# A two-layer transformer on one Trainium2 core: the first layer's feed-forward loads one per head, and sixteen matrix products whose results nobody reads

## What is computed

```python
x = x + L0_attn(layernorm(x))   # 16 heads of 128, rotary, signed weights (see below)
x = x + L0_ffn(layernorm(x))    # 16 experts, 4 per token, groups, plus a shared expert
x = x + L1_attn(layernorm(x))   # 16 heads of 16, rotary, softmax
x = x + L1_ffn(layernorm(x))    # 16 experts, 4 per token, plus a shared expert
# expert: silu(h @ g.T) * (h @ u.T) @ d.T, weighted by the routing weight of its token
```

## Time and profile before

| | us |
|---|---|
| median of 3 runs | 867.16 |
| lowest, highest run | 866.05, 870.68 |
| profiled execution | 864.81 |
| span of the profiled execution, first to last instruction | 863.1 |
| TensorE busy | 827.2 |

### The profile page before, as it was taken

One profiled execution on the slowest core, in us unless ns is written; L12 is line 12 of the kernel. 1 busy time (PEld: TensorE's weight loads), 2 busy tenths in 40 slices (PEclk: granted clock), 3 DMA queues, 4 the chain that ended last, 5 costly groups with the idle time before them and its releaser, 6 DMA issues.

```text
span 863.1 us, 14804 instructions
## 1 busy us (share of the span) xinstructions
PE 827.2 (96%) x4544; PEld 628.5 (73%) x4544; DVE 637.9 (74%) x1358; ACT 525.1 (61%) x1106; POOL 453.7 (53%) x391
## 2 busy tenths in 40 slices
PE   8899999999899999989998999999999989999997
PEld 7678888877688888866887888764444447888886
DVE  6798888888788888988476865768788644676553
ACT  4778788777678888863644533336566564454442
POOL 3555555555455556551666776623300426656774
PEclk9999999999999999999999999999999999999999
DMA  5232233333322333112665457412441122344451
GB/s 157 93 98 89 96 97 97 98 98 97 119 86 99 98 97 110 64 66 56 203 214 177 134 164 276 143 57 68 142 136 51 57 99 93 122 124 142 152 162 64
DMA packets 57442, 99.20 MB, mean 115 GB/s; under 512 B 8288, under 2 KB 19040, under 8 KB 57376
## 3 DMA queue, kind: packets, MB, share of 16 engines
q1 hardware_dynamic: 57376, 98.39, 35.7%
HBM read 71.88 MB, written 9.57 MB: 94 GB/s over the span
## 4 chain that ended last, share of the span: by engine, by line
PE 67%; DVE 10%; issue 9%; POOL 7%; ACT 3%; DMA 2%; SPq 0%; DVEq 0%; POOLq 0%; ACTq 0%
PE ps L993 10%; PE ps L979 9%; PE ps L970 9%; PE ps L321 7%; PE ps L387 5%; PE ps L335 5%; PE ps L348 4%; PE ps L375 3%; PE ps L362 3%; PE ps L1661 3%; POOL q_sin L542 2%; PE ps L1542 2%; PE ps L1631 2%; DVE nm L1853 2%; POOL wqk_lo L536 1%
## 5 line engine op out<-in xcount | busy, mean ns | idle before, releaser
L1117 POOL TENSOR_TENSOR ew_lo<-ew_raw,ew_hi 128x768 fp32r<-128x768 f32 x68 | 128.0, 1884 | 59.7 <-ACT ew_hi L1083 51.6
L1069 ACT ACTIVATE hid_hi<-guw 128x512 fp32r<-128x512 f32 x68 | 43.0, 632 | 156.5 <-POOL guw L1133 106.4
L1172 DVE TENSOR_TENSOR hid_lo<-guw,hid_hi 128x512 fp32r<-128x512 f32 x68 | 80.6, 1186 | 72.1 <-ACT hid_hi L1069 72.0
L1133 POOL TENSOR_TENSOR guw<-gu,cwb 128x512 f32<-128x512 f32 x61 | 80.4, 1318 | 91.1 <-issue 73.9
L542 POOL TENSOR_TENSOR q_sin<-q_sw,sin 128x512 f32<-128x512 f32 x62 | 80.4, 1305 | 79.6 <-DMA q_sw<-q_in 78.8
L1853 DVE TENSOR_REDUCE nm<-ps 128x1 f32<-128x512 f32 x128 | 81.3, 682 | 19.3 <-PE ps L1565 18.1
L1748 ACT ACTIVATE e<-ps 128x512 f32<-128x512 f32 x128 | 68.7, 602 | 35.2 <-PE ps L1661 35.0
L993 PE MATMUL ps<-ew_hi,hid_hi 128*128 128x256 f32 x272 | 78.3, 288 | 2.4 <-DVE hid_lo L1172 1.8
L497 DVE TENSOR_TENSOR q_rot<-ps,q_sin 128x512 f32<-128x512 f32 x64 | 43.9, 689 | 49.1 <-POOL q_sin L542 23.2
L438 ACT ACTIVATE ex<-sabs,nmax 128x512 f32<-128x512 f32 (+3 forms) x128 | 61.5, 553 | 28.2 <-DVE nmax L502 28.2
L993 PE MATMUL ps<-ew_lo,hid_hi 128*128 128x256 f32 x272 | 76.8, 283 | 0.0
(11 more groups left out here) (190 smaller groups left out, 2397.5 us busy)
## 6 DMA issues: line engine op xcount, KB each, us to landing
ew_raw<-in_ew SPq DMA_DIRECT2D x68, 384.0 KB, 3.5
q_sw<-q_in SPq DMA_DIRECT2D x128, 128.0 KB, 2.0
cwb<-cw_dram SPq DMA_DIRECT2D x61, 256.0 KB, 3.5
wqk_raw<-in_wqk SPq DMA_DIRECT2D x32, 256.0 KB, 2.7
wv_raw<-in_wv SPq DMA_DIRECT2D x32, 128.0 KB, 2.2
wo_raw<-in_wo SPq DMA_DIRECT2D x32, 128.0 KB, 2.2
qs<-stk_q SPq DMA_DIRECT2D x16, 256.0 KB, 3.7
ks<-stk_k SPq DMA_DIRECT2D x16, 256.0 KB, 4.1
```

The costliest lines, as they stand in the source:

```text
L1117: pool.tensor_tensor(ff[f].ew[1][:, i % EW_SLOTS, :], ew_raw[:, i % RAW_SLOTS, :], fp(ff[f].ew[0][:, i % EW_SLOTS, :]), ALU.subtract).then ...
L1133: pool.tensor_tensor(ff[f].guw[:, i % 2, :], ff[f].gu[:, i % 2, :], ff[f].cwb[:, r % CWB_SLOTS, :], ALU.mult).then_inc(sem("guw"), 1)
L1172: dve.tensor_tensor(ff[f].hid[1][:, i % 2, :], ff[f].guw[:, i % 2, :], fp(ff[f].hid[0][:, i % 2, :]), ALU.subtract).then_inc(sem("hid_lo"), 1)
```

## The change

The three small router transfers (`gw_raw`, `ebias`, `lower4`) are issued behind head 11 (H0 - 5) and not behind head 16; items 0, 1 and 2 are loaded behind heads 12, 13 and 14. For layer 1 `ffn_sp` does the same as before.

In layer 1's attention, sixteen `warm` products (128 rows, 128 columns, 512 moving columns, of `xT_hi`) are put in front of the score product of a slot: one in slot 3 of steps 21 to 24, three each in slots 1 and 2 of step 25, slot 2 of step 28 and slot 0 of step 29. Each group first waits, by `bank_wait`, for the bank that it writes: that of the slot's own maximum, of the transposed maxima (`taken`), of the logits (twice), and of the transposed routing weights (`cwT`).

```diff
         def a0_at_sp(sp, i):
-            if i == H0:
-                ffn_sp(sp, 0)
+            if i == H0 - 5:
+                ffn_sp_small(sp, 0)
+            if H0 - 4 <= i < H0 - 4 + RAW_SLOTS:
+                ew_load(sp, 0, i - (H0 - 4))
             if i == N0 - 3:
                 ew_load(sp, 0, RAW_SLOTS)
...
-        def ffn_sp(sp, f):
+        def ffn_sp_small(sp, f):
             sp.dma_start(gw_raw[:, :, :], a[f"gw{f}"]).then_inc(sem("gw_ld"), 16)
             sp.dma_start(ebias[:, :], a[f"ebias{f}"].partition_broadcast(P)).then_inc(sem("ebias_ld"), 16)
             sp.dma_start(lower4[:, :], a["lower4"].partition_broadcast(P)).then_inc(sem("ebias_ld"), 16)
+
+        def ffn_sp(sp, f):
+            ffn_sp_small(sp, f)
             for i in range(RAW_SLOTS):
                 ew_load(sp, f, i)
...
+        STEP_WARM = {(s, 3): ("max", HEADS * (s + LEAD) + 3) for s in (21, 22, 23, 24)}
+        STEP_WARM |= {(STEP_LOGIT, 1): ("taken", 7), (STEP_LOGIT, 2): ("logits", 0), (STEP_CWT, 2): ("cwT", 0),
+                      (STEP_CWT + 1, 0): ("logits", 0)}
...
                 for j in range(HEADS):
+                    if (s, j) in STEP_WARM:
+                        kind, n = STEP_WARM[s, j]
+                        bank_wait(pe, kind, n)
+                        warm(pe, 1 if kind == "max" else 3, BANK_OF[kind, n], half_of(xT_hi[:, 1, :], 1))
                     if HEADS * s + j + S_BANKS < HEADS * STEPS:
                         scores(HEADS * s + j + S_BANKS)
                     slot_pe(pe, s, j)
```

## The result

| | median of 20 runs (lowest to highest) | profiled execution | its span, mean granted clock |
|---|---|---|---|
| before | 870.83 us (861.31 to 876.05) | 864.81 us | 863.1 us |
| after | 864.67 us (860.60 to 867.33) | 863.15 us | 861.4 us, 0.996 |

The ratio is 0.9942, interval 0.9922 to 0.9962: 5.0 us faster (0.9942 x 870.83 = 865.8). The change is close to that; the time isn't: 864.67 was measured, and the kernel before is itself at 870.83 in more runs. That the change has the right size is luck: two errors stand against each other, as the traces show.

What follows compares the result with a forecast made beforehand. TensorE, busy 827.2 of 863.1 us, was taken as the bound, time lying in its idling and low clock. 864.81 - 5.44 + 0.4 + 0.1 - 0.3 = 859.6; 2.35 carried over less 0.8 gave 861.2 us, range 857.2 to 865.2.

Steps and rivals of the forecast that it cites:

- 5.44 us were to go: Head 17: moving the loads removes 3.62 us of TensorE idling before L321 and 1.82 us of slow clock.
- Four heads were to pay 0.4 in all: Heads receiving the moved loads: swaps delayed behind them cost 0.4 us together, at most 3.6 us.
- they only move their stall: Rival: the spread loads stall the earlier heads, costing 3.6 us instead of 0.4; 864.4 us, chance 0.12.
- another reason for head 17: Rival: head 17's wait is not the loads alone, two thirds of the 5.44 us stay; 864.8 us, chance 0.07.
- Steps 21 to 24, one product each: Layer 1 attention: four products cost 0.1 us, bounds 0 and 1.9, since TensorE runs ahead of DVE's maxima.
- this step gains 1.33 - 0.93 - 0.1 = 0.3 us: Step 25: full-clock logits gain 1.33 us; products and score on the path cost 0.93, those before slot 1 0.1.
- the products are exposed: Rival: all sixteen products stand in TensorE's way, 3.7 us, with no clock gained; 865.2 us, chance 0.08.
- The rule of the Trainium skill that I set aside: Step 25: idling between bursts lowers the clock, so products following a wait would not help; sum 2.3 us higher.
- several pieces: Argument against the rule: before the fall at 679 us TensorE idles 1.66 us in 7 us, but not in one stretch.
- I carry the 2.35 us over but for half such a fall, 0.8 us: Whole kernel: shown runs' median lies 2.35 us above the profiled execution; kept, less 0.8 us for clock falls avoided.
- in this execution they buy nothing either: Steps 28 and 29: six products fit into waits for ACT, cost nothing and gain nothing, the clock being full.
- signs of being right: Swaps landing in about 2 us, earlier heads keeping 11 us, logits about 1.4 us, ACT waits shrinking by 0.7 us.

Runs made afterwards that it cites:

- loads_only: The changed kernel without its sixteen products, only the loads moved; median 860.57 us, ratio 0.9906 to the kernel before, on chip 1.
- loads_only_b: The loads moved and no products, run again on chip 4; median 865.38 us, ratio 0.9943 to the kernel before.
- products_only: The kernel before with the sixteen products, loads behind head 16 as before; median 872.41 us, ratio 1.0019 to the kernel before.
- late_only: The kernel before with only the six products of steps 28 and 29, loads as before; median 868.66 us, ratio 0.9992 to the kernel before.
- after_again: The changed kernel unchanged, run again on chip 3; median 864.33 us, ratio 0.9913 to the kernel before.
- no_late: The changed kernel without the six products of steps 28 and 29; median 866.86 us, ratio 0.9978 to the kernel before.
- the first comparison: The changed kernel against the kernel before, 20 runs; medians 864.67 and 870.83 us, ratio 0.9942.
- pool_waits: The changed kernel, with GpSimd's first splits of layer 1's expert weights waiting for DVE's `nm_s`; median 860.41 us, ratio 0.9924 to the kernel before.

## Why the prediction was right or wrong

**The loads: right.** 5.44 us were to go, and head 17 gained 4.90: the 3.62 us of idling fell to 0.31 ("no more than 0.5" was to be left), and the clock gave back not 1.82 but 1.6 us, since the chain's 2.78 us begin after the first product of a run, and the timeline has 3.03 us for all twelve where the slow ones took 4.60. Four heads were to pay 0.4 in all, and that is what they pay: from the first L321 product after head 10 to that after head 16 pass 67.46 us on average in the thirteen profiles with all loads spread, and 67.10 in the four with the old loads. The profile of the kernel before alone hides it, as its 0.98 us of idling after head 13 are 0.36 to 0.39 in the other three. Without falls loads_only and loads_only_b gain 3.5 and 4.0 us, and head 17's fall on top. The rival that they only move their stall is out, as is another reason for head 17.

**Failed step: "Steps 21 to 24, one product each ... I take 0.1 us; if DVE's lead were gone, all of it would show."** About half of it shows: of four products at 0.43 us, 0.80 us (14.51 - 13.71). DVE's lead was too short to hide the rest, its last maximum waits 0.17 us for TensorE, and the maxima end 0.6 us later against GpSimd's chain, so that `nm_s` is held through all three splits in every profile with these products and no wait on GpSimd. I had priced the two rows of `nm_s` nowhere: 0.74 and 1.73 us for what takes 0.17 stood in the trace of before and were the sign of it.

**Failed step: step 25, "this step gains 1.33 - 0.93 - 0.1 = 0.3 us".** It loses. Three products and their score on the path are 678.96 - 677.64 = 1.32 us rather than 0.93: a 512-column product among products of other shapes isn't 2.78 / 12, since that row is the mean of a run of twelve alike. Their clock gain is not there: 3 falls in 6 profiles with them, 4 in 11 without. Against 6.51 us without a fall and without products, step 25 takes 7.83 with its six products and 8.94 with the held `nm_s` besides. The ten products of steps 21 to 25 together were to gain 0.2 us; they cost 0.80 + 2.43 = 3.2, which products_only's 3.1 confirms. That is the rival "the products are exposed" in size, by another way: the six late ones cost nothing.

The rule of the Trainium skill that I set aside ("TensorE: Matmul & The Clock Gate", section "Why this matters for your kernels"), which ties a fall to TensorE standing idle between bursts, has a case of its kind in late_only: the clock fell behind 2.36 us of idling in one piece, though that is shorter than the gap that the page names. With GpSimd's wait, which takes the cause of that idling away, it stayed up in all four profiles. But neither that rule nor my reading of "several pieces" settles it: in the changed kernel the waits for `nm_s` and `znT` were 0.76 and 1.09 us and the clock stayed up, and with the same products and like waits it fell in after_again, products_only and no_late. Nor does the rule cover the start of layer 1, where 13.7 us at half clock follow idle times of at most 0.48 us and 0.84 in all (7.00 - 6.16). What makes the clock fall stays open.

**Failed step: "I carry the 2.35 us over but for half such a fall, 0.8 us", and of steps 28 and 29 "in this execution they buy nothing either".** The offset goes with falls, as supposed, but it was carried over where it is much larger before than after: the medians of 20 runs lie 6.0 us above the profiled execution before and 1.5 after. The three runs shown could not tell the number of falls: 4.6 to 6.5 a run in the kernel before on the four chips, 2.4 to 2.8 in the changed kernel (in the first comparison the clocks of the kernel before are not on record). Three to four falls fewer, at 1.4 us each, are 4.2 to 5.6 us, where the sum had 0.8 and the 1.8 of head 17's. One of them is head 17's. The second quotation holds for the one execution, but the sum was for the median, and other executions lose clock in steps 28 and 29 (4 of 8 profiles without the late products). How the saved falls divide between the loads and the six late products stays open, since chip 1 and chip 4 differ.

For the changed kernel alone the offset came out as carried, 1.52 us for 1.55, by luck. So the 3.5 us by which 861.2 was too low lie in the sum for the profiled execution: 2.1 in steps 21 to 25 (1.93 lost, 0.2 gain forecast) and 1.75 in the fall at 611.8 us, less the 0.3 that the loads saved beyond the forecast.

The sum as measured: 3.5 to 4.0 us of work saved, 3.1 spent, 4 to 6 us of clock. These come from different chips, each good to about 1 us; the gains measured, 5.0 us at first and 6.2 between the medians on chip 3, fit them no more closely than that. Mine had 3.62 - 0.4 = 3.2 us saved, 0.2 gained by the products, and 1.82 + 0.8 = 2.6 us of clock. What the forecast named as signs of being right came true for the loads (of the four earlier heads one takes 12 us and not 11, as it does before), and the waits for ACT in steps 28 and 29 are gone; for step 25, logits of 1.49 us at full clock, on the chain, came true in this execution and not in after_again, and that is no sign of a gain.

## What to carry to other kernels

Read the mean granted clock of every run before the profile: where runs of one kernel differ by a percent, fit time against clock and judge a change by both numbers, the time without falls and the number of falls. Filler products belong where TensorE waits with nothing behind them on the path: six there cost nothing, and ten that stood on the path or delayed an engine with little lead cost 3 us. A short instruction that lasts many times its own time, and ends with one on another engine, points to a resource held by that other; ordering the two (here one wait) took 1.13 us off the step in the changed kernel and 0.75 without its ten products.

## What the runs showed that I had not expected

- GpSimd's split, two operands of 128 x 768, holds a DVE operation on 128 x 16 until it ends: 0.17 us becomes 0.74 to 4.27. The Trainium skill says so ("SBUF — State Buffer", section "Who interferes with whom": a DVE instruction with two inputs in SBUF and a GpSimd instruction that reads SBUF exclude each other), and these rows agree. `xT_lo`, with one input in PSUM, ran 1.27 us for two beside the third split of the kernel before, as in pool_waits (1.29); the maxima, which read PSUM, aren't held either.
- Who gets in between two splits isn't fixed: begun 1.11 to 1.13 us after the first, the first `nm_s` operation got in after it in six profiles, and in two (late_only, loads_only_b) it was held to the end of the third; its two operations then take 4.45 us instead of 2.49. What decides it stays open.
- Low clock comes in lengths of 3.4, 6.8, 10.2, 13.7 and 20.5 us, the longest at the start of layer 1 in products_only. There TensorE was busy for all of the 20.50 us.
